# Decoder on one core: four key projections moved from the end of the self-attention to behind the first two value projections of the masked attention

## The chip, the cores and the metric

One core of one Trainium2 chip runs the whole program in one launch. The metric is device microseconds (us) from start to end of an execution. TensorE (PE) has one in-order stream of matmuls, here in fp32: each matmul of the program shows as two records of the profile. PEld is its weight load, which overlaps it. The other engines are VectorE (DVE), ScalarE (ACT), GpSimd (POOL) and the DMA queue of SyncE (SP). They run side by side and wait for each other on semaphores.

## The reference

The program is a two-layer decoder on x (4 x 512 x 256). The part that matters is the first layer's two attentions, for each of four batches:

```python
# self-attention: 16 heads of 64, one zero key and value added
out = softmax(q @ [k;0].T * 64**-0.5) @ [v;0]
x = layernorm(x + out @ W_out + b_out)
# masked attention against ctx: 16 heads of 16
q = x @ Wq.T + bq + pos ;  k = ctx @ Wk.T + bk + pos ;  v = ctx @ Wv.T + bv
s = where(mask == 0, -1e9, q @ k.T / 4)
x = layernorm(x + softmax(s) @ v)
```

The keys and values of the masked attention depend on ctx alone, the queries on the layer norm between the two attentions. Behind these stand a mixture of 8 experts, a four-layer state-space stage, a second cross attention and a quantised gated network; none of their code is touched.

## The kernel before

All matrices lie in SBUF with the features on 128 partitions. One batch has T = 4 tiles of 128 tokens. A loop over the batches runs `attention(b)` and then `project(b + 1)`, which prepares the self-attention of the next batch. The order on each engine is written out by hand; semaphores tie the engines together.

The self-attention (`attend` with AT_A, 32 steps, one tile of two heads each) is a pipeline: scores on TensorE (L1196), maximum on VectorE, exponentials on ScalarE, scaling on GpSimd (L672), transposes on TensorE (L1209, called LAG = 3 steps later), copies of the transposed halves by VectorE (L1660) and ScalarE (L837), and the value products (L1231), which need four transposed steps each. VectorE copies a bank of output out with L1709, and the attention on TensorE ends with a wait for the last of these.

`attend` takes a function `between`. TensorE calls it right after the last transposes and ahead of the last four value products (the last group). Before the change this is `keys`, which issues the four key projections of the masked attention:

```python
if k == n and between is not None:
    between()
```

`pj` (L1169) is a projection: two matmuls over 512 tokens into one of banks 0 to 3, copied out by ScalarE (L812, Identity with a bias). `tm` (L1177) is a projection with tokens on the partitions, into bank 4 or 5 in turn, and waits for the copy out of the unit before the last:

```python
if u >= 2:
    pe.wait_ge(tm_ev, TM(b, u) - 1)
```

After the self-attention TensorE issues four output projections (TM_AO, 8 matmuls each), whose results VectorE adds to x_in (L1728), then the four value projections of the masked attention (TM_BV, 2 matmuls each), numbered BV0 to BV3 below, then eight transposes of the normalised x (`tr`, L1162), and then the four query projections (PJ_BQ). VectorE adds the bias (L1730), runs the layer norm `ln(b, 0)` (L1630, L1634, L1637, L1640), and only then copies the value projections out (L1734). ScalarE's part of the norm is one square root (L816), preceded by a load of its function table, as the exponentials use another table. BV2 waits for the copy of BV0, BV3 for that of BV1.

SP starts the load of the mask (L500) when the self-attention's value products are done, and the loads of the next batch's x and ctx (L484, L485) when the four output projections have been copied out. Neither waits for the keys.

Of the kernel before, what the change touches and what calls it, by code (L numbers as in the profile page):

```python
# [35 lines left out]
PJ_A, PJ_BK, PJ_BQ, PJ_EK, PJ_EV, PJ_EQ, PJ_L1, PJ_N = 0, 16, 20, 24, 26, 28, 30, 38  # L36
# [3 lines left out]
AT_A, AT_B, AT_E, AT_N = 0, 32, 64, 80  # L40
OT_A, OT_B, OT_E, OT_N = 0, 8, 12, 14
# [62 lines left out]
def place(count, b, u, m):  # L104
    return count(b, u) % m if isinstance(b, Two) else u % m
# [37 lines left out]
def decoder(nc, d, out):  # L143
# [11 lines left out]
    with ExitStack() as ctx:  # L155
# [104 lines left out]
        def wv(at, kc, n):  # L260
            return AR[:, at:at + kc * n].rearrange("p (c n) -> p c n", c=kc)
# [4 lines left out]
        CT = ar([P, KC, S])  # L266
# [3 lines left out]
        probs = ar([P, 4, 2, 512])  # L270
        pT = [ar([P, 2, 4, 512]) for k in range(2)]
        a_qT = ar([P, 8, 512])
        b_kT_at = ar.at
        a_kT = ar([P, 8, 512])
# [9 lines left out]
        a_V = ar([P, T, F])  # L284
# [158 lines left out]
        wbq, wbk, wbv = wv(W_BQ, KC, 512), wv(W_BK, KC, 512), wv(W_BV, KC, D)  # L443
# [349 lines left out]
        def _(act):  # L793
# [10 lines left out]
            def tr_ev(u, dst, base):  # L804

                act.wait_ge(tr_ps, TR(base, u) + 1)
                act.activation(dst, PS[:, 6, :].rearrange("p (t q) -> p t q", q=P)  # L807
                               if len(dst.shape) == 3 else PS[:, 6, :], ACT.Copy).then_inc(tr_a, 1)

            def pj(b, u, dst, func=ACT.Copy, scale=1.0, bias=0.0):  # L810
                act.wait_ge(pj_ps, PJ(b, u) + 1)
                act.activation(dst, PS[:, place(PJ, b, u, 4), :], func, bias=bias, scale=scale).then_inc(pj_ev, 1)  # L812

            def ln(b, i):
                act.wait_ge(ln_mv, LN(b, i) + 1)
                act.activation(std[:], mv[:, :, 1], ACT.Sqrt, bias=epsc[:, 0:1]).then_inc(ln_std, 1)  # L816

            def attend(b, at, n, src, per, probs, pT):
                s0, g0 = AT(b, at), GT(b, at // 4)
                def exps(i):  # L820
                    s = s0 + i
                    act.wait_ge(smax, s + 1)
                    if i >= 4:
                        act.wait_ge(pt_ps, s - 3)
                        act.wait_ge(den_ok, s - 3)
                    for q in range(2):
                        ins = act.activation(probs[:, i % 4, q, :], src(i, q), ACT.Exp, scale=-1.0 if at == AT_B else 1.0,  # L827
                                             bias=nm[:, i % 4, q:q + 1], accum_out=sm[:, i % 4, q:q + 1])
                    if per == 2:
                        ins = act.activation(e0[:, i % 4, :], nm[:, i % 4, :], ACT.Exp)  # L830
                    ins.then_inc(probs_ok, 1)

                def copy(k):
                    act.wait_ge(pt_ps, s0 + k + 1)
                    if k % 4 == 0 and k >= 8:
                        act.wait_ge(av, g0 + k // 4 - 1)
                    act.activation(part_of(pT, k, 1, per), PS[:, 5, :].rearrange("p (c q) -> p c q", q=P), ACT.Copy).then_inc(pt_a, 1)  # L837

                for i in range(n + LAG):
                    if at == AT_B and i % 2 == 0:  # L840
                        for k in (i - LAG, i - LAG + 1):
                            if 0 <= k < n:
                                copy(k)
                    if i >= LAG and at != AT_B:
                        copy(i - LAG)
                    if i < n:
                        exps(i)
# [17 lines left out]
            def attention(b):  # L865
                attend(b, AT_A, 32, lambda i, q: PS[:, 2 * (i % 2) + q, :], 2, probs, pT)
                for c in range(4):
                    pj(b, PJ_BK + c, b_kT[:, c, :], ACT.Identity, bias=cols[:, C_BK + c:C_BK + c + 1])
                ln(b, 0)
                tr_ev(TR_LNA, XT[:, 0, :], b)  # L870

                for c in range(4):
                    pj(b, PJ_BQ + c, b_qT[:, c, :], ACT.Identity, 0.25, cols[:, C_BQ + c:C_BQ + c + 1])
                attend(b, AT_B, 32, lambda i, q: b_S[:, i % 2, q, :], 4, probs, pT)
                ln(b, 1)
                tr_ev(TR_LNB, XT[:, 0, :], b)

            project(0)
            with act.Fori(0, B - 1) as b:
                attention(b)  # L880
                project(b + 1, b)
            attention(B - 1)
            gate_exp(B - 1)

# [265 lines left out]
        def _(pe):  # L1150
# [3 lines left out]
            def tr(b, u, src, c0=0, ln=None):  # L1154
                if u:
                    pe.wait_ge(tr_a, TR(b, u))
                    pe.wait_ge(tr_v, TR(b, u))
                for t in range(T):
                    if ln is not None:
                        pe.wait_ge(ln_out, LN(b, ln) * T + t + 1)  # L1160
                    for c in range(KC):
                        ins = pe.transpose(PS[:, 6 + c, t * P:(t + 1) * P], src[:, t, (c0 + c) * P:(c0 + c + 1) * P], ident[:])  # L1162
                ins.then_inc(tr_ps, 1)

            def pj(b, u, w, xT, c, kc=KC, p0=0):
                if u - p0 >= 4 or isinstance(b, Two):
                    pe.wait_ge(pj_ev, PJ(b, u) - 3)
                for k in range(kc):
                    ins = pe.matmul(PS[:, place(PJ, b, u, 4), :], w[:, k, c * P:(c + 1) * P], xT[:, k, :],  # L1169
                                    start=k == 0, stop=k == kc - 1)  # L1170
                ins.then_inc(pj_ps, 1)

            def tm(b, u, xT, t, w, kc=KC, n0=0, n=D):
                if u >= 2:
                    pe.wait_ge(tm_ev, TM(b, u) - 1)
                for k in range(kc):
                    ins = pe.matmul(PS[:, 4 + place(TM, b, u, 2), 0:n], xT[:, k, t * P:(t + 1) * P], w[:, k, n0:n0 + n],  # L1177
                                    start=k == 0, stop=k == kc - 1)
                ins.then_inc(tm_ps, 1)
# [91 lines left out]
            def attention(b):  # L1271
                pe.wait_ge(pj_ev, PJ.one(b, PJ_BK))
                pe.wait_ge(tm_ev, TM.one(b, TM_AO))
                pe.wait_ge(ld_b, 64)

                def keys():
                    for c in range(4):
                        pj(b, PJ_BK + c, wbk, CT, c)

                attend(b, AT_A, 32, a_qT, a_kT, a_V, 2, OT_A, False, probs, pT, keys)  # L1280
                for t in range(T):
                    tm(b, TM_AO + t, a_oT, t, waout, kc=FC)

                for t in range(T):
                    tm(b, TM_BV + t, CT, t, wbv)
                tr(b, TR_LNA, X, ln=0)
                pe.wait_ge(tr_a, TR.one(b, TR_LNB))
                pe.wait_ge(tr_v, TR.one(b, TR_LNB))

                for c in range(4):  # L1290
                    pj(b, PJ_BQ + c, wbq, XT, c)
                pe.wait_ge(pj_ev, PJ.one(b, PJ_EK))
                pe.wait_ge(tm_ev, TM.one(b, TM_EV))
                attend(b, AT_B, 32, b_qT, b_kT, b_V, 4, OT_B, True, probs, pT)
                for t in range(T):
                    for m in range(4):
                        ins = pe.transpose(PS[:, t, m * P:(m + 1) * P], b_oT[:, m, t * P:(t + 1) * P], ident[:])
                    ins.then_inc(bo_ps, 1)
                tr(b, TR_LNB, X, ln=1)
                pe.wait_ge(tr_a, TR.one(b, TR_CB))  # L1300
                pe.wait_ge(tr_v, TR.one(b, TR_CB))

                for t in range(T):
                    for k in range(KC):
                        ins = pe.matmul(PS[:, 4, t * NE:(t + 1) * NE], XT[:, k, t * P:(t + 1) * P], gateW[:, k, :],
                                        start=k == 0, stop=k == KC - 1)
                ins.then_inc(gate_ps, 1)

            project(0)
            with pe.Fori(0, B - 1) as b:  # L1310
                attention(b)
                project(b + 1, b)
            attention(B - 1)
            rank(B - 1)
            pe.wait_ge(wred_ok, 1)
# [916 lines left out]
```

## Time and profile before

| | us |
|---|---|
| median of 3 runs | 4511.87 (4507.68 to 4519.54) |
| profiled execution | 4511.59 |
| span in its profile | 4509.9 |
| mean granted TensorE clock | 0.934 |
| TensorE busy | 3857.7 |
| VectorE busy | 3081.9 |
| key projections start, batches 0 to 3 | 169.73, 479.23, 789.82, 1098.88 |
| query projections start, batches 0 to 3 | 207.16, 517.47, 828.07, 1136.00 |

Times in rows are microseconds from the start of the span. A row of the timeline gives start, length, engine, line of the kernel, operation, output and input, count, and in brackets the idle time of the engine before it and who ended it. Ends of matmuls are modelled, so starts are the better marks.

### The profile page before, as it was taken

The page shows a single profiled execution, that of the slowest core. Times are in us where ns is not written, and L with a number is a line of the kernel's source. Part 1 is how long each engine was busy: PE and PEld are TensorE (multiplying, and loading weights), DVE is VectorE, ACT ScalarE, POOL GpSimd, SP SyncE. Part 2 cuts the span into 40 slices and gives each one's busy share as a digit, 9 for nine tenths or more (in the row PEclk, how much of TensorE's full clock was granted, in tenths as well). Part 3 has the DMA queues.
Part 4 walks back from the last instruction along what each step waited for, and adds up shares of the span by engine and source line. Part 5 has one row for each costly group of instructions (what it writes and reads, how often), then busy time and mean ns, then how long its engine had stood idle before and what let it go on. Part 6 is the DMA issues. An engine that isn't in the chain of part 4 may idle for free.

```text
span 4509.9 us, 47995 instructions
## 1 busy us (share of the span) xinstructions
PE 3857.7 (86%) x15752; PEld 2038.4 (45%) x15760; DVE 3081.9 (68%) x4131; ACT 2302.7 (51%) x4201; POOL 2285.2 (51%) x1206
## 2 busy tenths in 40 slices
PE   7879889789769995799999999999999987887786
PEld 3444444444459993233333333433333333444443
DVE  3566447446631112599999999999999998546646
ACT  4455455445622222666667666666666663332432
POOL 2354345334500003578888787778887785230220
PEclk9999999999979997899999999999999999788788
DMA  6000000000068883011111111111111120000000
GB/s 223 19 6 11 19 15 2 19 15 10 1 254 317 314 315 113 26 35 34 48 34 40 36 48 33 40 36 34 48 36 38 36 91 25 8 10 10 10 1 10
DMA packets 102383, 272.99 MB, mean 61 GB/s; under 512 B 9776, under 2 KB 55728, under 8 KB 96400
## 3 DMA queue, kind: packets, MB, share of 16 engines
q1 hardware_dynamic: 97216, 256.75, 16.5%
q0 software_dynamic: 4944, 13.51, 0.9%
q8 instruction: 110, 1.80, 0.2%
q14 instruction: 113, 0.93, 0.1%
HBM read 237.32 MB, written 32.90 MB: 60 GB/s over the span
## 4 chain that ended last, share of the span: by engine, by line
PE 37%; DVE 18%; POOL 18%; issue 16%; ACT 9%; SPq 1%; DMA 0%; POOLq 0%; another core or an unknown queue 0%; DVEq 0%; ACTq 0%
POOL AR L672 11%; DVE AR L1940 8%; PE PS L1450 8%; PE PS L1337 6%; DVE PS L1934 4%; PE PS L1393 4%; POOL AR L773 3%; PE PS L1347 3%; PE PS L1364 3%; PE PS L1169 3%; ACT AR L1035 2%; PE PS L1177 2%; PE PS L1196 2%; PE PS L1209 2%; PE PS L1443 1%
## 5 line engine op out<-in xcount | busy, mean ns | idle before, releaser
L773 POOL TENSOR_TENSOR AR<-AR 128x1024 f32<-128x1024 f32 x512 | 1217.6, 2384 | 414.8 <-DVE AR L1940 338.4
L1940 DVE TENSOR_TENSOR_SCAN AR<-AR,PS 128x1024 f32<-128x1024 f32 x512 | 1170.4, 2286 | 17.6
L672 POOL TENSOR_TENSOR AR<-AR,rden 128x1024 f32<-128x1024 f32 x320 | 606.2, 1895 | 1002.0 <-DVE rden L1671 935.1
L1450 PE MATMUL PS<-AR,ident 128*128 128x512 f32 x2048 | 1024.6, 628 | 33.4 <-POOL AR L773 33.3
L1035 ACT ACTIVATE AR<-AR,mcol 128x511 f32<-128x511 f32 x1024 | 668.1, 712 | 140.9 <-DVE AR L1940 138.6
L1934 DVE TENSOR_TENSOR PS<-AR,PS 128x1024 f32<-128x1024 f32 x512 | 627.9, 1226 | 79.0 <-PE PS L1435 60.0
L1450 PEld LDWEIGHTS PS<-AR,ident 128*128 128x128 f32 x2048 | 371.6, 194 | 481.1 <-issue 413.5
L1209 PE MATMUL PS<-ident,AR 128*128 128x128 f32 x2560 | 379.4, 295 | 107.0 <-POOL AR L672 92.1
L1209 PEld LDWEIGHTS PS<-ident,AR 128*128 128x128 f32 x2560 | 299.6, 150 | 354.0 <-POOL AR L672 221.8
L1196 PE MATMUL PS<-AR 32*128 32x512 f32 (+1 forms) x1280 | 318.3, 710 | 45.1 <-ACT e L830 11.7
L837 ACT ACTIVATE AR<-PS 128x512 f32<-128x512 f32 x320 | 189.7, 593 | 302.5 <-PE PS L1209 301.8
L827 ACT ACTIVATE AR<-PS,nm 128x512 f32<-128x512 f32 x384 | 259.6, 685 | 95.5 <-DVE nm L1696 74.0
L1169 PE MATMUL PS<-AR 128*128 128x512 f32 x608 | 284.7, 627 | 13.2 <-ACT AR L807 4.5
L1364 PE MATMUL PS<-AR 128*128 128x512 f32 x512 | 260.5, 633 | 39.5 <-ACT AR L1013 24.1
L1337 PE MATMUL PS<-AR 128*128 128x128 f32 x2496 | 286.9, 276 | 8.5 <-ACT AR L893 8.5
L1337 PEld LDWEIGHTS PS<-AR 128*128 128x128 f32 x2496 | 286.6, 193 | 10.9 <-ACT AR L893 8.9
L1660 DVE COPY AR<-PS 128x512 f32<-128x512 f32 x320 | 219.9, 687 | 86.5 <-PE PS L1209 85.5
L1177 PE MATMUL PS<-AR 128*128 128x256 f32 (+1 forms) x896 | 236.6, 424 | 32.5 <-DVE AR L1734 18.0
L1231 PE MATMUL PS<-AR 128*32 128x256 f32 (+1 forms) x2048 | 256.1, 452 | 2.3 <-DVE AR L1660 1.2
L1393 PE MATMUL PS<-AR 128*128 128x512 f32 x512 | 242.3, 596 | 6.3 <-ACT AR L939 4.0
L1882 DVE TENSOR_TENSOR AR<-PS,AR 128x512 f32<-128x512 f32 x78 | 54.0, 692 | 271.0 <-ACT AR L902 271.0
L1689 DVE CUSTOM_DVE_ANT_0 AR<-PS,AR 128x512 f32<-128x512 f32 x256 | 169.4, 683 | 102.0 <-PE PS L1196 98.2
(259 smaller groups left out, 4682.5 us busy)
## 6 DMA issues: line engine op xcount, KB each, us to landing
AR<-in_xw SPq DMA_DIRECT2D x39, 3072.0 KB, 10.5
AR<-mid_cs SPq DMA_DIRECT2D x256, 256.0 KB, 3.3
mid_xs<-AR SPq DMA_DIRECT2D x32, 512.0 KB, 7.7
AR<-mid_xs SPq DMA_DIRECT2D x39, 128.0 KB, 9.6
mid_ys<-AR POOLq DMA_DIRECT2D x39, 128.0 KB, 7.9
AR<-in_ctx SPq DMA_DIRECT2D x8, 512.0 KB, 4.9
AR<-in_mask SPq DMA_DIRECT2D x4, 1024.0 KB, 5.4
mid_x<-AR SPq DMA_DIRECT2D x8, 512.0 KB, 3.0
```

The lines of the kernel that those rows point to most:

```text
L672: pool.tensor_tensor(probs[:, i % 4], probs[:, i % 4], rden[:, i % 4, :].rearrange("p (q o) -> p q o", o=1).to_broadcast([P, 2, 512]), ALU ...
L773: pool.tensor_tensor(m_HC[:, W % 3], m_H[:, W % 3, :].rearrange("p (c s) -> p c s", c=2), m_cb[:, n % 4:n % 4 + 1, :].to_broadcast([P, 2, ...
L1035: ins = act.activation(m_dA[:, W % 4, c, 1:512], m_dl[i % 2][:, cc, 1:512], ACT.Exp, scale=mcol[:, i // B, at:at + 1])
L1169: ins = pe.matmul(PS[:, place(PJ, b, u, 4), :], w[:, k, c * P:(c + 1) * P], xT[:, k, :], start=k == 0, stop=k == kc - 1)
L1196: ins = pe.matmul(PS[:, 2 * (e % 2) + q, :], qT[r:r + wide, h // per, t * P:(t + 1) * P], kT[r:r + wide, h // per, :], start=True, stop=True)
L1209: ins = pe.transpose(PS[:, 4 + q, c * P:(c + 1) * P], probs[:, k % 4, q, c * P:(c + 1) * P], ident[:])
L1337: ins = pe.matmul(PS[:, bank, f * P:(f + 1) * P], w[:, kc, f0:f0 + P], x_T[:, kc, :], start=kc == 0, stop=kc == KC - 1)
L1364: ins = pe.matmul(bank, mWin[:, k, c * P:(c + 1) * P], m_hT[:, k, :], start=k == 0, stop=k == KC - 1)
L1393: ins = pe.matmul(bank, dgc[:, 4 * c + k, :], m_xi[:, c, k:k + 512], start=k == 0, stop=k == 3)
L1450: ins = pe.matmul(PS[:, 2 * hf + c, :], ident[:], m_HC[:, W % 3, c, :], start=False, stop=n == NS - 1)
L1934: v.tensor_tensor(PS[:, 4:6, :], m_du[i % 2][:, 2 * hf:2 * hf + 2, :], PS[:, 6:7, :].to_broadcast([P, 2, 512]), ALU.mult).then_inc(d_bx, 1)
L1940: v.tensor_tensor_scan(m_H[:, W % 3, :], m_dA[:, W % 4].rearrange("p c s -> p (c s)"), PS[:, 4:6, :].rearrange("p c s -> p (c s)"), 0.0, A ...
```

## The change

TensorE no longer issues the four key projections within the self-attention. It issues them between BV1 and BV2. ScalarE, whose order must match, copies out the first key projection, then does its part of the layer norm, then copies out the other three.

```diff
@@ scalar: attention(b)
                 for c in range(4):
                     pj(b, PJ_BK + c, b_kT[:, c, :], ACT.Identity, bias=cols[:, C_BK + c:C_BK + c + 1])
-                ln(b, 0)
+                    if c == 0:
+                        ln(b, 0)
                 tr_ev(TR_LNA, XT[:, 0, :], b)
@@ tensor: attention(b)
-                def keys():
-                    for c in range(4):
-                        pj(b, PJ_BK + c, wbk, CT, c)
-
-                attend(b, AT_A, 32, a_qT, a_kT, a_V, 2, OT_A, False, probs, pT, keys)
+                attend(b, AT_A, 32, a_qT, a_kT, a_V, 2, OT_A, False, probs, pT)
                 for t in range(T):
                     tm(b, TM_AO + t, a_oT, t, waout, kc=FC)
 
                 for t in range(T):
                     tm(b, TM_BV + t, CT, t, wbv)
+                    if t == 1:
+                        for c in range(4):
+                            pj(b, PJ_BK + c, wbk, CT, c)
                 tr(b, TR_LNA, X, ln=0)
```

## Rows read from the trace of the kernel before

**Rows 1.** The page: span, busy time and share of each engine.
```profile
span 4509.9 us, 47995 instructions
PE 3857.7 (86%) x15752; PEld 2038.4 (45%) x15760; DVE 3081.9 (68%) x4131; ACT 2302.7 (51%) x4201; POOL 2285.2 (51%) x1206
```

**Rows 2.** Waits, 168 to 216 us (batch 0): total, times, longest.
```profile
DVE AR L1709 <- PE PS L1231: 10.3, 2, 10.0
PE PS L1177 <- DVE AR L1734: 4.5, 1, 4.5
```

**Rows 3.** Timeline of batch 0, end of the self-attention.
```profile
168.72 1.08 PE L1231 MATMUL PS<-AR 128*64 128x512 f32 x4
168.83 0.69 DVE L1660 COPY AR<-PS 128x512 f32<-128x512 f32 x1 [1.50 <-PE PS L1209]
169.73 7.13 PE L1169 MATMUL PS<-AR 128*128 128x512 f32 x16
171.75 0.69 ACT L812 ACTIVATE AR<-PS,cols 128x512 f32<-128x512 f32 x1 [2.33 <-PE PS L1169]
173.47 0.69 ACT L812 ACTIVATE AR<-PS,cols 128x512 f32<-128x512 f32 x1 [1.03 <-PE PS L1169]
176.80 3.65 PE L1231 MATMUL PS<-AR 128*64 128x512 f32 x16
180.50 0.69 DVE L1709 COPY AR<-PS 128x512 f32<-128x512 f32 x1 [9.96 <-PE PS L1231]
```

**Rows 4.** Timeline of batch 0, output projections to query projections.
```profile
181.32 15.80 PE L1177 MATMUL PS<-AR 128*128 128x256 f32 x72 [0.87 <-DVE AR L1709]
185.07 0.42 DVE L1728 TENSOR_TENSOR AR<-PS,AR 128x256 f32<-128x256 f32 x1 [3.88 <-PE PS L1177]
188.53 0.42 DVE L1728 TENSOR_TENSOR AR<-PS,AR 128x256 f32<-128x256 f32 x1 [3.03 <-PE PS L1177]
199.12 0.30 ACT L816 ACTIVATE std<-mv,epsc 128x4 f32<-128x4 f32 x1 [20.22 <-DVE mv L1634]
201.17 0.76 DVE L1734 TENSOR_TENSOR AR<-PS,AR 128x256 f32<-128x256 f32 x2
201.65 3.26 PE L1177 MATMUL PS<-AR 128*128 128x256 f32 x8 [4.53 <-DVE AR L1734]
207.16 7.13 PE L1169 MATMUL PS<-AR 128*128 128x512 f32 x16 [0.97 <-DVE AR L1621]
```

**Rows 5.** Windows, batch 0: PE, PEld, DVE, ACT, POOL busy, granted clock, DMA share, GB/s.
```profile
198.00:202.00 4.00, 0.35 (x2) 0.33 (x3) 3.25 (x13) 0.30 (x1) 0.00 (x0) 1.00 0.71 245
202.00:206.00 4.00, 4.00 (x16) 3.28 (x14) 0.85 (x2) 0.00 (x0) 0.00 (x0) 0.57 0.00 0
...
124.00:168.00 44.00, 43.63 (x232) 19.67 (x232) 33.17 (x73) 27.57 (x80) 27.76 (x15) 1.00 0.00 1
```

**Rows 6.** Timeline of batches 1 and 3, the same stretch.
```profile
511.14 3.78 PE L1177 MATMUL PS<-AR 128*128 128x256 f32 x8 [4.52 <-DVE AR L1734]
517.47 7.13 PE L1169 MATMUL PS<-AR 128*128 128x512 f32 x16 [0.96 <-DVE AR L1621]
1130.63 3.67 PE L1177 MATMUL PS<-AR 128*128 128x256 f32 x8 [4.43 <-DVE AR L1734]
1134.13 1.04 PE L1162 MATMUL PS<-ident,AR 128*128 128x128 f32 x8
1136.00 7.10 PE L1169 MATMUL PS<-AR 128*128 128x512 f32 x16 [0.83 <-ACT AR L807]
```

**Rows 7.** Timeline of ScalarE around another table load.
```profile
340.80 0.60 ACT L812 ACTIVATE AR<-PS 128x512 f32<-128x512 f32 x1 [1.12 <-PE PS L1169]
341.41 1.28 ACT L862 ACT_TABLE_LOAD   x1
342.70 0.23 ACT L862 ACTIVATE g_t<-g_t 128x32 f32<-128x32 f32 x1
```

**Rows 8.** Line L1169, start to 225 us: ns min/median/max of a record.
```profile
L1169 PE MATMUL PS<-AR x96: 592/592/1192, 20.8 to 213.7; 128*128 128x512 f32 x96
```

## The prediction

> **What bounds the kernel now.** I read the page first [rows 1]: TensorE is the busiest engine with 86% of the span, but that is an average over five very different stages, so it says nothing yet about this change. The chain that ended last is no help in this stretch either: it puts the 52 us between two scalings of GpSimd down to "issue". So I went to the waits of the stretch from the end of one attention to the start of the next, then to its timeline, in which the order can be followed.
>
> The waits show two places where an engine stands still for long behind another [rows 2]: VectorE 10.0 us for TensorE, ahead of the last copy of the self-attention's output, and TensorE 4.5 us for VectorE, ahead of BV2.
>
> The first is explained by the timeline [rows 3]. The last transposed half is copied by VectorE from 168.83 for 0.69 us, to 169.52. That is all that the last group of value products needs, and TensorE has issued the group before it by then. But at 169.73 it starts the keys, 16 records that take until 176.80, and only then the last value products. VectorE's copy, the output projections, the layer norm and everything behind them stand behind that group. So the keys are wholly on the path here, though no one needs them before the next attention. Batches 0 to 3 repeat it alike; the row of batch 0 stands for four.
>
> The second is in the next stretch [rows 4]. TensorE starts the output projections at 181.32. Their results are copied out 3.45 us apart (185.07, 188.53), which is 16 records, so a record costs 0.216 us. The group has 72 records (64 of the output projections, 8 of BV0 and BV1), so TensorE has issued it all at 181.32 + 72 x 0.216 = 196.85. I call this moment T0. BV2 starts at 201.65, T0 + 4.80, because VectorE copies BV0 out only behind the layer norm. The whole rest is one chain: ScalarE's root at 199.12, normalisation, copy of BV0 from 201.17, BV2, BV3, transposes, queries at 207.16.
>
> The clock belongs to it [rows 5]. While TensorE is idle, from 198 to 202 us, the granted clock is still 1.00; in the next 4 us it is 0.57, so it has fallen to the lower of its two levels, 1.2 GHz, behind an idle of 4.5 us. The 8 records of BV2 and BV3, which would take 1.73 us, take over 3 us. From the start of BV2 to the start of the queries it is 5.51 us in batch 0, 6.33 us in batch 1 [rows 4, 6], as much in batch 2, and 5.37 us in batch 3 (1130.63 to 1136.00), on average 5.9 us.
>
> **What goes away.** The keys leave the path at the end of the self-attention: 176.80 - 169.73 = 7.07 us per batch. What else could hold the last value products there? Only the two copies of transposed halves, over at 169.52, and TensorE's own order. The idle from such a copy to a matmul behind it is small: BV2 starts at 201.65 behind a copy that begins at 201.17 and takes 0.42. So the group starts between 169.6 and 169.8, and the saving is between 7.0 and 7.15 us; I take 7.07. Nothing reads the keys until the masked attention, and there is no DMA in the part that moves: 8 matmuls (16 records, 16 weight loads) and 4 copies on ScalarE. Of SP's queue, the mask's load is released by the end of the value products and so comes 7 us earlier, as its reader does; the loads of x and ctx follow the output projections and shift with them.
>
> **What is added.** The keys now start at T0 instead of an idle of 4.8 us. I take the same 7.07 us for them, so BV2 starts at T0 + 7.07 if TensorE sets it. I check the other chain, since ScalarE's root now stands behind the copy of the first key. That copy starts 2.02 us behind the first key record (171.75 against 169.73) and takes 0.69, the table load behind it 1.28, so the root can start at T0 + 4.0, against T0 + 2.27 before. From the root to BV2 it was 201.65 - 199.12 = 2.53 us. VectorE would so release BV2 at T0 + 6.5: the norm comes 1.7 us later than before, and this is hidden under the keys with only 0.5 us to spare. Behind ScalarE's root wait the copies of keys 1 to 3; they come 1.72 us apart and no one waits for them but the masked attention. The copies use Identity, and in the timeline the query copies, which stand behind the root, run without a table load in front of them, so none is added. VectorE's copies of BV0 and BV1, and the normalised x for the transposes, are in time by the same sum.
>
> The clock pays a part back. TensorE has no idle from the output projections to BV2, so I expect it to stay at 2.4 GHz. BV2 and BV3 then take 8 x 0.216 = 1.73 us, and from the transposes to the queries it is 1136.00 - 1134.13 = 1.87 us, from batch 3, in which the transposes already ran fast [rows 6]. That is 3.60 us instead of 5.9.
>
> The sum of this stretch from T0 to the queries: before 4.8 + 5.9 = 10.7 us; after 7.07 + 3.60 = 10.67 us. The keys fit into the idle and the clock's loss, and cost nothing. What is left is the 7.07 us of the first place, four times: 28.3 us. If that cover were gone, that is, with the clock low from BV2 on, the second stretch would take 7.07 + 5.9 = 12.97 us, and 2.3 us per batch come back.
>
> What a switch of ScalarE's table costs is seen in full at another place [rows 7]: a copy ends at 341.40, the load starts at 341.41 and takes 1.28 us, and the function starts at 342.70, so nothing but the load itself lies between. A rule of the Trainium skill speaks against this reckoning. The Trainium skill (ScalarE: Activation LUTs, "What ACT_TABLE_LOAD costs") adds a drain of about 1.38 us to every switch. By it the root would start at T0 + 5.4 and BV2 at T0 + 7.9, 0.8 to 0.9 us behind the keys, and the sum would be some 25 us. Rows 7 contradict it for this kernel.
>
> **The rivals.**
>
> *The clock falls anyway* behind the keys. For it: it fell in all four batches at this place, and is low again early in the masked attention. Against: it fell behind an idle that is now filled. Time: 4 x (7.07 - 2.3) = 19.1 us gained, 4492.5.
>
> *ScalarE's root becomes the bound*, since it stands behind a copy and a table load that used to be long done. For it: only 0.5 us are to spare, on modelled ends. Against: rows 7. If the switch costs the length of a second load, 1.28 us, BV2 comes 0.8 us late: 28.3 - 3.2 = 25.1 us gained, 4486.5. The drain of the Trainium skill's page, above, would be one way to this case.
>
> *The change doesn't shorten the path*: the last value products wait for something that the keys hide. The seven us would turn up as idle ahead of L1231. Against: both copies are over at 169.52. No change, 4511.6.
>
> *Slower*: the low clock comes earlier, ahead of or in the keys. They are 7 us of unbroken matmul, which now no longer stand ahead of the output projections, where TensorE idles for 0.87 us. Against: from 124 to 168 us TensorE is busy for 43.6 of 44 us at clock 1.00 [rows 5], and at 1.00 through the output projections. A record of a projection takes 592 ns, and up to 1192 in the slow level [rows 8], twice as much. With all keys at half clock they cost 6.9 us more, with BV2 to the queries at the old 5.9: 13.97 + 5.9 = 19.9 against 10.7, 9.2 lost against 7.07 won, 2.1 us worse per batch, 4520. It decides from the point where some 7 us of full-clock work run at half clock; were part of the output projections slow too, each 3.45 us of them would cost as much again.
>
> **How the numbers follow.** The profiled execution is 4511.59 us for a span of 4509.9, and the median of the three runs is 4511.87, so the sum can be made against either: 4511.6 - 28.3 = 4483.3. The likeliest case has 74 in 100. Its own range is some 6 us to either side: the placing of the clock's falls later in the layer differs from batch to batch (queries of batch 2 to those of batch 3 are 307.9 us apart, others 310.3 and 310.6, so it is worth up to 2.7 us a batch), and the runs before lie 12 us apart. The clock falling anyway 8, ScalarE's root 6, no change 4, the slower case 8, half of it within 0.3%. A measurement of this kernel can tell about 0.3% (13.5 us) from nothing. The first three are faster: 88 in 100; within 0.3%: 8; slower: 4. The range for 8 in 10 goes from 4475 to 4496, and takes in the first three.
>
> **What would show it.** In the profile after, L1231's last group starts about 1 us behind the group before it, and VectorE's wait ahead of the last L1709 falls from 9.96 us to about 2.9. L1177's group of BV2 shows no idle of 4.5 us; L1169 x16 stands in front of it. The root L816 starts about 4 us behind the keys' start, directly behind its table load, which now lies behind the first key copy. The clock from BV2 to the queries is 1.00, and BV2 to queries takes 3.6 us. The queries of batches 0 to 3 start earlier by about 7, 14, 21 and 28 us. The prediction is wrong if BV2 waits visibly for VectorE, if the clock is 0.5 to 0.6 in these 4 us, or if an idle appears ahead of the last L1231.

## The result and the profile after

The changed kernel takes 4484.32 us (median of 4 runs, 4481.83 to 4489.70), beside 4515.70 us (4507.68 to 4519.95) of the kernel before. The medians are 31.4 us apart. The ratio on record is 0.9938, with a 95% interval from 0.9922 to 0.9955. It is not the quotient of the two medians (0.9931), but the interval holds both. By the ratio the change is worth 28 us (20 to 35), so the gain is clear of noise. The forecast was 4483.3. Its span is 26.8 us shorter:

```profile
span 4483.1 us, 48003 instructions
```

The timeline of batch 0 answers to [rows 3] and [rows 4]. In the changed file the line numbers of TensorE are one higher (L1196 is L1197, L1169 is L1170, L1177 is L1178, L1162 is L1163), and the value products are L1232. In the other runs they move by a few lines too.

```profile
167.08 4.69 PE L1232 MATMUL PS<-AR 128*64 128x512 f32 x20
168.21 0.69 DVE L1709 COPY AR<-PS 128x512 f32<-128x512 f32 x1 [0.33 <-PE PS L1232]
171.82 0.69 DVE L1709 COPY AR<-PS 128x512 f32<-128x512 f32 x1 [2.92 <-PE PS L1232]
...
172.64 15.80 PE L1178 MATMUL PS<-AR 128*128 128x256 f32 x72 [0.86 <-DVE AR L1709]
...
188.28 7.03 PE L1170 MATMUL PS<-AR 128*128 128x512 f32 x16
...
190.20 0.69 ACT L812 ACTIVATE AR<-PS,cols 128x512 f32<-128x512 f32 x1 [22.41 <-PE PS L1170]
190.90 1.28 ACT L816 ACT_TABLE_LOAD   x1
192.20 0.30 ACT L816 ACTIVATE std<-mv,epsc 128x4 f32<-128x4 f32 x1
...
194.25 0.76 DVE L1734 TENSOR_TENSOR AR<-PS,AR 128x256 f32<-128x256 f32 x2
195.15 1.89 PE L1178 MATMUL PS<-AR 128*128 128x256 f32 x8
...
196.88 1.04 PE L1163 MATMUL PS<-ident,AR 128*128 128x128 f32 x8
...
198.88 7.13 PE L1170 MATMUL PS<-AR 128*128 128x512 f32 x16 [0.96 <-DVE AR L1621]
```

Read it from the top. The last two groups of value products now run as one piece of 20 records: nothing stands between them. VectorE's wait for the last one is 2.92 us, against 9.96 in [rows 3]: 7.04 us less. T0, the moment at which TensorE has issued BV1, is 172.64 + 15.53 = 188.17 (15.53 us are 72 records of 3.45 / 16 us, as in the prediction), and the keys start at 188.28. BV2 starts at 195.15, T0 + 6.98, with no idle in brackets, against 201.65 and 4.53 us of idle in [rows 4]. From BV2 to the queries it is 3.73 us instead of 5.51. ScalarE's root starts directly behind its table load, and that directly behind the copy of the first key.

The granted clock, which was 0.57 from 202 to 206 us in [rows 5], is 1.00 in the same part of the work:

```profile
192.00:196.00 4.00, 4.00 (x12) 2.09 (x11) 2.32 (x7) 2.40 (x5) 0.00 (x0) 1.00 0.06 18
196.00:200.00 4.00, 3.04 (x16) 2.16 (x15) 2.67 (x4) 0.63 (x2) 0.00 (x0) 1.00 0.01 4
```

The four batches, from the start of the output projections to the first scores of the masked attention, in us, worked out from the starts in the timelines:

| batch | 0 | 1 | 2 | 3 | sum |
|---|---|---|---|---|---|
| before | 33.82 | 34.64 | 34.65 | 33.50 | 136.61 |
| changed | 34.22 | 34.22 | 34.22 | 33.99 | 136.65 |

So eight matmuls per batch, 7 us of TensorE, were added to this stretch for 0.04 us in all. Before, the stretch differs by up to 1.2 us between batches, by where the clock fell and rose; now it hardly does.

**The balance of the span.** At the end of the self-attention 7.04 us were won in three batches (VectorE's wait falls from 9.96 to 2.92 us) and 7.19 in the last (to 2.77): 28.3 us. Batch 0 also reached this point 1.6 us earlier in the profiled execution (the start of the output projections is 8.68 us earlier, the change explains 7.04). That makes 29.9 us, and 26.8 were seen. Two rows have the rest. From the first masked scores to the root of the second norm batch 0 took 105.6 us (206.86 to 312.48) against 103.7 before (215.14 to 318.86), 1.9 us more. And the transposes behind the second norm ran at the slow clock from their start in batches 1 and 2, 0.56 us more each. Both are places where the clock is low for some us in either kernel, and the runs below, `after_again` above all, bear on whether the change is the cause.

### The profile page after: what moved, and what is told of

Its sections match the earlier page's. It is cut to its first block, busy times and chain, and to the rows that moved or that the text cites. A ratio compares the mean times of both kernels' runs of the same rounds, so it can differ in the third digit from the quotient of the medians.

```text
span 4483.1 us, 48003 instructions
## 1 busy us (share of the span) xinstructions
PE 3851.2 (86%) x15760; PEld 2035.4 (45%) x15760; DVE 3082.2 (69%) x4131; ACT 2302.9 (51%) x4201; POOL 2285.0 (51%) x1206
## 4 chain that ended last, share of the span: by engine, by line
PE 37%; POOL 18%; DVE 18%; issue 15%; ACT 9%; SPq 1%; DMA 0%; POOLq 0%; DVEq 0%; ACTq 0%
POOL AR L672 11%; PE PS L1450 8%; DVE AR L1940 7%; PE PS L1337 6%; DVE PS L1934 4%; PE PS L1393 4%; POOL AR L773 3%; PE PS L1347 3%; PE PS L1364 3%; PE PS L1170 3%; ACT AR L1036 3%; PE PS L1178 2%; PE PS L1197 2%; PE PS L1210 2%; PE PS L1443 1%
## 5 line engine op out<-in xcount | busy, mean ns | idle before, releaser
L1197 PE MATMUL PS<-AR 32*128 32x512 f32 (+1 forms) x1280 | 317.3, 709 | 45.0 <-ACT AR L827 11.5
L1170 PE MATMUL PS<-AR 128*128 128x512 f32 x608 | 285.1, 627 | 13.2 <-ACT AR L807 4.5
L1232 PE MATMUL PS<-AR 128*32 128x256 f32 (+1 forms) x2048 | 255.8, 452 | 2.3 <-DVE AR L1660 1.2
L1178 PE MATMUL PS<-AR 128*128 128x256 f32 (+1 forms) x896 | 229.7, 415 | 14.5 <-DVE AR L1709 5.0
```

What stands on the lines that cost most here:

```text
L1197: ins = pe.matmul(PS[:, 2 * (e % 2) + q, :], qT[r:r + wide, h // per, t * P:(t + 1) * P], kT[r:r + wide, h // per, :], start=True, stop=True)
```

## The experiments

A ratio is always to the kernel before on the same chip, as the chips differ: the kernel before has a median of 4503.3 us beside keys_twice, keys_out, root_last and two_moved, 4510.5 beside warm_norm, key_behind, root_first and warm_both, and 4502.5 beside first_behind, best and after_again. An interval of 0.9920 to 0.9953 is 15 us wide, so differences of a few us are read from the rows.

| run | median us | ratio (95% interval) |
|---|---|---|
| changed kernel | 4484.32 | 0.9938 (0.9922 to 0.9955) |
| keys_twice | 4505.42 | 1.0005 (0.9995 to 1.0015) |
| keys_out | 4474.25 | 0.9937 (0.9920 to 0.9953) |
| root_last | 4502.14 | 0.9997 (0.9988 to 1.0007) |
| two_moved | 4485.10 | 0.9963 (0.9949 to 0.9977) |
| warm_norm | 4473.99 | 0.9921 (0.9898 to 0.9945) |
| key_behind | 4482.59 | 0.9932 (0.9909 to 0.9955) |
| root_first | 4484.39 | 0.9942 (0.9921 to 0.9962) |
| warm_both | 4466.98 | 0.9905 (0.9883 to 0.9928) |
| first_behind | 4473.71 | 0.9938 (0.9921 to 0.9954) |
| best | 4448.92 | 0.9879 (0.9863 to 0.9896) |
| after_again | 4475.45 | 0.9943 (0.9926 to 0.9959) |

### keys_twice: the new place alone

```diff
                     tm(b, TM_BV + t, CT, t, wbv)
+                    if t == 1:
+                        pe.wait_ge(pj_ev, PJ.one(b, PJ_BQ))
+                        for c in range(4):
+                            for k in range(KC):
+                                pe.matmul(PS[:, c, :], wbk[:, k, c * P:(c + 1) * P], CT[:, k, :],
+                                          start=k == 0, stop=k == KC - 1)
```

> The kernel before, with the eight key matmuls issued a second time between BV1 and BV2, into the same banks, their results unused. Only the second place is tested. Theory (the 7 us fit into an idle of 4.8 us plus the 2.2 us that the clock gives back): T0 to the queries 10.7 us as before, the whole within 2 us of before, clock 1.00 from BV2 to the queries. Rival 1 (only the idle counts, the clock would stay low behind the keys too): 2.3 us more per batch, 9 us slower. Rival 2 (matmuls put there simply cost their 7 us): 28 us slower.

Eight more matmuls per batch, 28 us of work in all, change the time by a ratio of 1.0005, and by 7 us at the most (1.0015). The timeline shows why; L1290 are the repeated keys:

```profile
197.22 7.03 PE L1290 MATMUL PS<-AR 128*128 128x512 f32 x16
...
204.09 1.89 PE L1177 MATMUL PS<-AR 128*128 128x256 f32 x8
205.82 1.04 PE L1162 MATMUL PS<-ident,AR 128*128 128x128 f32 x8
207.82 7.13 PE L1169 MATMUL PS<-AR 128*128 128x512 f32 x16 [0.96 <-DVE AR L1627]
```

BV2 starts 2.2 us later than the idle would allow, and makes this good by 3.73 us instead of 5.9 to the queries. From the output projections to the masked scores it is 34.22, 34.22, 34.21 and 33.99 us, as in the changed kernel. Rival 1, by which the clock gives nothing back, would need 2.3 us more in each. In this kernel the path ahead is the old one, so the new place is shown to be free by itself: the four stretches take 136.6 us, as they do before.

### keys_out: the old place alone

```diff
                     if t == 1:
-                        for c in range(4):
-                            pj(b, PJ_BK + c, wbk, CT, c)
+                        pe.sem_inc(pj_ps, 4)
```

> The changed kernel without the eight key matmuls anywhere: TensorE only counts up the semaphore between BV1 and BV2, ScalarE still copies four (stale) banks, so the masked attention uses wrong keys. Theory (moved keys are free): the idle of 4.8 us and the low clock behind it come back, T0 to the queries 10.3 to 11.1 us as before the change, the whole within 3 us of the changed kernel's 4484. Rival 1 (the keys overfill the idle and the clock is high either way): 8.5 instead of 10.7 us per batch, 8.7 us faster than the changed kernel, 4476. Rival 2 (the keys cost their 7 us in the new place): 28 us faster, 4456.

This kernel leaves the keys out, so its masked attention works with wrong ones. The ratio is 0.9937, that of the changed kernel. As far as the interval tells, to leave the keys out altogether brings no more than to move them. The idle and the slow clock are back:

```profile
194.76 3.78 PE L1178 MATMUL PS<-AR 128*128 128x256 f32 x8 [4.52 <-DVE AR L1733]
198.33 1.90 PE L1163 MATMUL PS<-ident,AR 128*128 128x128 f32 x8
201.20 7.13 PE L1170 MATMUL PS<-AR 128*128 128x512 f32 x16 [0.96 <-DVE AR L1620]
```

BV2 to the queries is 6.44 us here, and from the output projections to the masked scores it is 34.74, 34.75, 34.71 and 33.50 us: a little more, on average, than with the keys in place.

### root_last: how late the norm may be

```diff
                     pj(b, PJ_BK + c, b_kT[:, c, :], ACT.Identity, bias=cols[:, C_BK + c:C_BK + c + 1])
-                    if c == 0:
-                        ln(b, 0)
+                ln(b, 0)
```

> The changed kernel with ScalarE's old order: all four key copies, then the square root of the layer norm. Theory (the norm is hidden under the keys with 0.5 us to spare, and becomes the bound as soon as it is later): the root starts at T0 + 9.3 us instead of T0 + 4.0, BV2 at T0 + 11.8 behind an idle of some 4.8 us, the clock falls behind it, 5.9 instead of 3.7 us to the queries: 7 us more per batch, 28 us more than the changed kernel, 4512, as much as before the change. Rival (ScalarE's order does not matter, since only TensorE's order makes the gain): 4484. Rival 2 (the idle comes, but the clock stays high): 4.8 us per batch, 4503.

The whole gain is gone, with TensorE's order as in the changed kernel: ratio 0.9997.

```profile
196.76 1.28 ACT L816 ACT_TABLE_LOAD   x1
198.06 0.30 ACT L816 ACTIVATE std<-mv,epsc 128x4 f32<-128x4 f32 x1
...
200.59 3.55 PE L1177 MATMUL PS<-AR 128*128 128x256 f32 x8 [4.56 <-DVE AR L1733]
...
206.10 7.13 PE L1169 MATMUL PS<-AR 128*128 128x512 f32 x16 [0.96 <-DVE AR L1620]
```

T0 is 173.35 + 15.53 = 188.88, so the root starts at T0 + 9.2 and BV2 at T0 + 11.7, as reckoned. The idle of 4.56 us brings the slow clock back: from BV2 to the queries it is 5.5 us in batch 0, against 3.73 in the changed kernel. The stretch to the masked scores is 40.74, 41.67, 41.61 and 40.41 us, 6.9 us more per batch than in the changed kernel and 27.8 in the four. So without the change's move on ScalarE, the move on TensorE gains nothing.

### root_first: whether the root is the bound

```diff
-                for c in range(4):
-                    pj(b, PJ_BK + c, b_kT[:, c, :], ACT.Identity, bias=cols[:, C_BK + c:C_BK + c + 1])
-                    if c == 0:
-                        ln(b, 0)
+                ln(b, 0)
+                for c in range(4):
+                    pj(b, PJ_BK + c, b_kT[:, c, :], ACT.Identity, bias=cols[:, C_BK + c:C_BK + c + 1])
```

> The changed kernel with ScalarE's root ahead of all four key copies. Theory (TensorE's keys set BV2, the root had 0.5 us to spare): the root starts at T0 + 2.3 instead of T0 + 4.0, nothing behind BV2 moves, the time is that of the changed kernel, 4484. Rival (BV2 was held by VectorE's chain after all): BV2 earlier than T0 + 6.9, up to 2 us per batch faster.

```profile
192.16 0.30 ACT L816 ACTIVATE std<-mv,epsc 128x4 f32<-128x4 f32 x1 [21.36 <-DVE mv L1633]
...
196.86 1.89 PE L1177 MATMUL PS<-AR 128*128 128x256 f32 x8
```

The output projections start at 174.36, so T0 is 189.89: the root is at T0 + 2.3, 1.8 us earlier than in the changed kernel, and BV2 at T0 + 6.97, as there. The stretch to the masked scores is 34.22, 34.22, 34.22 and 33.99 us, and the ratio 0.9942. The rival, an earlier BV2, did not occur: in the changed kernel the keys set BV2, and the root is hidden.

### key_behind and first_behind: how much is to spare

The first moves key 3 behind the transposes:

```diff
                     if t == 1:
-                        for c in range(4):
+                        for c in range(3):
                             pj(b, PJ_BK + c, wbk, CT, c)
                 tr(b, TR_LNA, X, ln=0)
+                pj(b, PJ_BK + 3, wbk, CT, 3)
```

with ScalarE's copy of key 3 behind `tr_ev(TR_LNA, ...)`. The second also puts the root ahead of all key copies.

> The changed kernel with key 3 behind the transposes of the normalised x, where TensorE idles 0.97 us for their copies; keys 0 to 2 between BV1 and BV2. Theory (keys beyond the idle cost their full time): BV2 at T0 + 5.3 instead of T0 + 7.0, key 3 fills the 0.97 us and costs some 0.8 more, so T0 to the queries 9.8 instead of 10.7: 0.9 us per batch, 3.6 us faster than the changed kernel, 4480, too little for the time to tell but plain in the rows. Rival (VectorE's chain releases BV2 only at T0 + 6.5, as the root stands behind the first key copy): BV2 at T0 + 6.5, and T0 to the queries 11.0, 1 us slower than the changed kernel.

```profile
193.09 0.30 ACT L816 ACTIVATE std<-mv,epsc 128x4 f32<-128x4 f32 x1
...
195.62 1.99 PE L1179 MATMUL PS<-AR 128*128 128x256 f32 x8 [1.13 <-DVE AR L1736]
```

My own theory missed and its rival held. T0 is 189.07; BV2 starts at T0 + 6.55 behind an idle of 1.13 us for VectorE, not at T0 + 5.3. From the output projections to the masked scores it is 34.38 us, 0.16 more than in the changed kernel, and 0.8 us more over the four batches, where the rival had 1. With a shorter filling the root behind the first key copy is the bound at once. That also measures what the prediction had as 0.5 us to spare: 6.98 - 6.55 = 0.43 us.

> Key 3 behind the transposes of the normalised x, and ScalarE's root ahead of all key copies. Theory (VectorE's chain released BV2 at T0 + 6.55 when key 3 stood behind alone, because the root stood behind a key copy): the root starts at T0 + 2.3, BV2 at T0 + 5.3, set by three keys, T0 to the queries 9.8 instead of 10.7 us, 0.9 us per batch, 3.6 us in all. Rival (something else holds BV2): BV2 at T0 + 6.5, no gain.

```profile
191.83 0.30 ACT L816 ACTIVATE std<-mv,epsc 128x4 f32<-128x4 f32 x1 [21.36 <-DVE mv L1635]
...
194.82 1.89 PE L1178 MATMUL PS<-AR 128*128 128x256 f32 x8
```

T0 is 189.56, BV2 at T0 + 5.26 without idle, and the stretch to the masked scores is 32.99 us in three batches and 32.92 in the last, 1.2 us less than in the changed kernel, where 0.9 was expected. By the time (4473.71 beside 4475.45 of the changed kernel on the same chip) this can't be told from nothing; only the rows show it. The 4.7 us of the four batches are in part taken back later: batches 1 and 2 took 105.6 us from the first masked scores to the second root, 1.6 more each than in after_again.

### two_moved: an idle that is partly filled

```diff
                 def keys():
-                    for c in range(4):
+                    for c in range(2):
                         pj(b, PJ_BK + c, wbk, CT, c)
...
                     tm(b, TM_BV + t, CT, t, wbv)
+                    if t == 1:
+                        for c in range(2, 4):
+                            pj(b, PJ_BK + c, wbk, CT, c)
```

> Keys 0 and 1 stay at the end of the self-attention, keys 2 and 3 move between BV1 and BV2; ScalarE takes the root between the copies of key 1 and key 2. Theory: 3.5 us leave the first place; in the second, two keys fill 3.5 of 4.8 us, an idle of 1.3 us is left, behind which the clock stays high: T0 to the queries 4.8 + 3.7 = 8.5 us against 10.7, so 2.2 us more are won there. Together 5.7 us per batch, 23 us faster than before, 4489 to 4492. Rival (the clock falls behind 1.3 us of idle too): only the 3.5 us, 14 us faster than before, 4501. Rival 2 (half the keys, half of the gain) gives the same 14 us but by other rows; the clock from BV2 to the queries tells.

```profile
169.97 3.70 PE L1170 MATMUL PS<-AR 128*128 128x512 f32 x8
...
173.60 3.65 PE L1232 MATMUL PS<-AR 128*64 128x512 f32 x16
...
198.45 1.99 PE L1178 MATMUL PS<-AR 128*128 128x256 f32 x8 [1.09 <-DVE AR L1738]
200.28 1.04 PE L1163 MATMUL PS<-ident,AR 128*128 128x128 f32 x8
202.28 7.13 PE L1170 MATMUL PS<-AR 128*128 128x512 f32 x16 [0.96 <-DVE AR L1625]
```

At the place itself the theory holds: two keys cost 3.63 us ahead (169.97 to 173.60), 3.44 us less than the four in [rows 3], an idle of 1.09 us is left, and the clock behind it is high (transposes 1.04 us, granted clock 1.00 from 198 to 206 us). The stretch is 32.14 us in two batches, 32.18 and 31.82, on average 2.1 us less than before or in the changed kernel. That adds up to 22 us. The time shows 17 (0.9963, that is 10 to 23 us), between the two expectations. In its profile the first masked scores to the second root took 105.25 us in batch 3 instead of 104.0, and of the gain 4 us are missing between the second root of one batch and the output projections of the next (170.96, 169.28 and 167.44 us, against 171.96, 171.88 and 170.26 before, less 3.44 each). The slow clock stands there for a while in every kernel here. So the rows decide between the expectations, and the time alone would not.

### after_again: the changed kernel on another chip

> The changed kernel as it is, once more, for a second profile on another chip. Theory (what differed by 1.9 us between the queries of batch 0 and the second norm was the place where the low clock fell, not the change): T0 to the queries 10.7 us in all batches again, and the 1.6 us gone or in another batch. Rival (it belongs to the change): 105.6 us from the first masked scores to the second root in batch 0 again.

The ratio is 0.9943. The stretch is 34.21, 34.22, 34.21 and 33.99 us again. From the first masked scores to the second root it is 104.06, 104.04, 104.04 and 104.01 us: the 105.6 of the first profile is gone. Across the kernels with this stretch of code untouched the value is 103.7, 104.0 to 104.1, 105.3 or 105.6 us, in differing batches. The granted clock in the 25 us from the first masked scores goes with it. It is 0.73 in batch 0 of the first profile (105.6 us), 0.80 in its batch 1 (104.1), and 0.86 in batch 0 of the kernel before (103.7), the last line:

```profile
207.00:232.00 25.00, 17.48 (x104) 9.53 (x104) 14.76 (x45) 15.94 (x39) 12.99 (x7) 0.73 0.00 1
512.00:537.00 25.00, 16.93 (x110) 9.68 (x103) 16.00 (x49) 15.56 (x39) 13.35 (x8) 0.80 0.01 1
...
215.10:240.10 25.00, 17.23 (x116) 9.45 (x120) 15.76 (x49) 16.22 (x40) 13.34 (x8) 0.86 0.00 1
```

It is 0.73 too in batches 1 and 2 of first_behind (105.6 us) and in batch 3 of two_moved (105.3), 0.80 in batch 0 of after_again (104.1), and 0.86 in batch 3 of root_last (103.7). So the 1.9 us of batch 0 come from how long the low clock lasts there, which differs between profiles of one kernel, and not from the change. The second row of the balance moved too: the 0.56 us behind the second norm stand in batches 0 and 1 here instead of 1 and 2, and in keys_twice in batches 0, 1 and 2. The kernel before has them in none; whether the change makes them more frequent, one profile of it can't tell.

### warm_norm, warm_both and best: the same reasoning elsewhere

The times between places here and below are worked out from the starts in the timelines. If work in an idle is free and keeps the clock, then matmuls whose results no one uses should gain time by themselves. The place is the second norm of the changed kernel:

```profile
313.49 1.41 PE L1163 MATMUL PS<-ident,AR 128*128 128x128 f32 x8 [3.48 <-DVE AR L1640]
315.84 3.55 PE L1305 MATMUL PS<-gateW,AR 128*128 128x8 f32 x16 [0.94 <-DVE AR L1621]
319.25 1.95 PE L1163 MATMUL PS<-ident,AR 128*128 128x128 f32 x8
322.46 1.94 PE L1163 MATMUL PS<-ident,AR 128*128 128x128 f32 x8 [1.27 <-ACT AR L853]
325.62 8.76 PE L1170 MATMUL PS<-AR 128*128 128x512 f32 x16 [1.22 <-ACT AR L807]
```

Behind 3.48 us of idle the clock is 0.50 from 316 to 328 us.

```diff
                     ins.then_inc(bo_ps, 1)
+                for c in range(4):
+                    pe.matmul(PS[:, 5, :], ident[:], CT[:, c % 2, :], start=True, stop=True)
```

> The changed kernel with four filler matmuls (ident by CT into bank 5, results unused, 8 records, some 3.4 us) behind the output transposes of the masked attention, in TensorE's idle of 3.5 us for the second layer norm. The same reasoning at a second place, without any gain from a shorter path. Theory (a filled idle keeps the clock): in the changed kernel the granted clock is 0.5 for some 14 us behind this idle (transposes 1.97 us for 8, gate 3.55, transposes 1.95 and 1.94, first queries and keys of the next batch 8.76 instead of 7.13). With the clock at 1.00 this is worth 5 to 6 us in each of three batches and 2 in the last: 15 to 20 us faster than the changed kernel, 4464 to 4469. Rival (the clock falls behind the later idles of 0.9 to 1.3 us anyway): the first transposes only, 1 us per batch, 4480. Rival 2 (filler is late work and delays the transposes): slower by up to 1 us per batch.

```profile
315.95 1.92 PE L1307 MATMUL PS<-gateW,AR 128*128 128x8 f32 x16 [0.94 <-DVE AR L1623]
317.72 1.07 PE L1163 MATMUL PS<-ident,AR 128*128 128x128 f32 x8
320.06 1.94 PE L1163 MATMUL PS<-ident,AR 128*128 128x128 f32 x8 [1.27 <-ACT AR L853]
323.22 10.01 PE L1170 MATMUL PS<-AR 128*128 128x512 f32 x16 [1.22 <-ACT AR L807]
```

Gate and first transposes are fast now, but the next transposes and the projections are not: 1.94 us as before, and 10.01 instead of 8.76. The granted clock of this run shows where it falls, behind the idle of 0.94 us and as that of 1.27 us begins:

```profile
314.00:318.80 4.80, 3.85 (x31) 3.16 (x30) 1.96 (x7) 0.60 (x1) 0.00 (x0) 1.00 0.32 113
318.80:329.00 10.20, 7.71 (x15) 4.09 (x16) 2.74 (x15) 2.77 (x5) 0.00 (x0) 0.50 0.00 0
```

From the second root to the next output projections batches 0 to 2 win 1.5, 1.7 and 3.3 us, 6.6 together, not 15. On the same chip it is 10 us faster than root_first, whose TensorE does the changed kernel's work. That lies between the expectation (15 to 20 us) and its rival (some 4). Much of the slow stretch only moved on.

warm_both adds three more behind the first scores of the masked attention:

```diff
                         scored(i)
+                        if i == 0:
+                            for c in range(3):
+                                pe.matmul(PS[:, 7, :], ident[:], CT[:, c % 2, :], start=True, stop=True)
```

> As the kernel with filler in the second norm, and three more filler matmuls (2.6 us, bank 7) behind the first scores of the masked attention, where TensorE idles 2.8 us. Theory (the clock falls for this idle): the low clock in the first 20 us of the masked attention goes or is shorter; from the queries to the output transposes it was 109.2 us in batch 0 and 107.6 in batches 1 and 2 of the changed kernel; 1 to 3 us per batch less, 4 to 12 us in all beside the other filler. Rival (later idles of 1 to 3 us in the filling of the pipeline lower the clock as well, or GpSimd's scaling sets the pace anyway): no more than 1 us per batch.

```profile
207.30:211.30 4.00, 3.20 (x13) 1.38 (x14) 1.86 (x7) 2.48 (x3) 0.00 (x0) 1.00 0.00 0
211.30:215.30 4.00, 2.63 (x17) 1.09 (x16) 2.21 (x10) 2.41 (x8) 2.72 (x2) 1.00 0.01 2
215.30:219.30 4.00, 3.12 (x15) 2.17 (x17) 2.76 (x7) 3.65 (x10) 2.39 (x2) 0.59 0.00 0
```

The clock stays high for 8 us behind the first masked scores and then falls to 0.59 all the same, later than in the changed kernel. The first masked scores to the second root take 103.2, 104.6, 103.2 and 101.7 us instead of 105.6, 104.1, 104.1 and 104.1: 5 us in all, and 7 by the medians of warm_norm and warm_both. Against the usual 104.05 us it is less: 0.9, -0.6, 0.9 and 2.4 us. So only batch 3 gains what was expected (1 to 3 us), two batches stay below it, as the rival had it, and batch 1 loses.

`best` adds to the last two the order of first_behind, and one filler each in the idles to which the slow clock had moved:

```diff
                 tr(b, TR_LNB, X, ln=1)
+                pe.matmul(PS[:, 5, :], ident[:], CT[:, 0, :], start=True, stop=True)
...
                 tr(b, TR_X, x_in)
+                if prior is not None:
+                    pe.matmul(PS[:, 5, :], ident[:], CT[:, 0, :], start=True, stop=True)
                 tr(b, TR_C, ctx_tok)
+                if prior is not None:
+                    pe.matmul(PS[:, 5, :], ident[:], XT[:, 0, :], start=True, stop=True)
```

> As the kernel with the root first and key 3 behind, with filler matmuls (results unused) in all idle places found: four in the second norm, three behind the first masked scores, and one each ahead of the gate, between the transposes of the next x and ctx, and ahead of the next projections. Theory (with filler in the second norm alone the low clock only moved to the next idles of 0.9 to 1.3 us; filled too, it goes): clock 1.00 from the second norm to the end of the next projections, transposes 1.04 us instead of 1.94, first projections 7.13 instead of 8.6 to 10.0, 4 us more in each of three batches; with the other parts 15 us less than the kernel with two fillers, ratio to before 0.987. Rival (a filler that misses its idle is work on the path): each costs up to 0.9 us, and the time stays at the ratio 0.990.

```profile
314.98 1.07 PE L1163 MATMUL PS<-ident,AR 128*128 128x128 f32 x8
...
317.32 1.07 PE L1163 MATMUL PS<-ident,AR 128*128 128x128 f32 x8 [0.41 <-ACT AR L853]
...
319.60 7.11 PE L1170 MATMUL PS<-AR 128*128 128x512 f32 x16 [0.36 <-issue]
```

The projections take 7.11 us, the transposes 1.07, and the granted clock is 1.00 in every window of 4 us from 300 to 328 us. From the second root to the next output projections it is 160.2, 160.6 and 158.3 us, against 164.9, 165.4 and 163.7 in the changed kernel. The ratio is 0.9879, where 0.987 was expected and 0.990 by the rival. That is 26.5 us less than the changed kernel on the same chip (4448.92 beside 4475.45), and 24.8 less than first_behind, from which it differs by the fillers alone: 10 matmuls more per batch (8 in the last) whose results no one reads.

## Why the prediction was right

**What goes away** was put at 7.07 us per batch; the wait of VectorE shows 7.04 and in the last batch 7.19. It rested on the reading that the value products wait only for copies over by 169.52 and for TensorE's own order. That they now follow the group before without a gap shows it, and keys_out gets the same gain without any keys.

**What is added** was BV2 at T0 + 7.07; it came at T0 + 6.98. The root was put at T0 + 4.0 and came at T0 + 4.03; VectorE's release of BV2 was put at T0 + 6.5, and key_behind measured T0 + 6.55. The rival of ScalarE's root was so near because 0.43 us were all there was to spare, and root_last shows what it would have cost in full: the whole gain.

**The clock** was to pay back 2.3 us per batch: 3.60 us from BV2 to the queries instead of 5.9; it was 3.73 in three batches and 3.59 in the last. The prediction took its 1.87 us from the transposes to the queries from batch 3, and in the others it is 2.00. BV2 comes 0.09 us earlier than reckoned, which makes up for most of that: T0 to the queries was put at 10.67 us, and is 10.70. The rival that it falls anyway is excluded by the windows of the changed kernel, and keys_twice shows this term apart from the first one: 28 us of added work, ratio 1.0005. The slower rival, a low clock ahead of the keys or in them, did not occur: the output projections take 15.80 us as before, and the keys 6.87 us from their start to BV2.

**The table switch.** The load at 190.90 starts when the copy ends and the root follows 0.02 us behind it. The drain of about 1.38 us that the Trainium skill (ScalarE: Activation LUTs, "What ACT_TABLE_LOAD costs") adds is not seen in this place either, and the trace disagrees with that figure here: the root starts at T0 + 4.03, not at T0 + 5.4.

**The sum** of 28.3 us stands beside 26.8 in the span, 28 by the ratio and 31.4 between the medians. The queries start 8.3, 13.8, 20.7 and 26.8 us earlier; about 7, 14, 21 and 28 were forecast. What the sum left out, the place of the slow clock later in the layer, was -3.0 us, against 1.6 us by which batch 0 came earlier. By after_again the 1.9 us of batch 0 are not the change's; for the 1.1 us behind the second norm that is likely and not shown. The start of batch 0 differs as much within one kernel: its output projections start at 172.64 us in the first profile and at 175.16 in after_again. That these terms nearly cancel is luck, and so is the median within 1 us of the forecast, as the four runs of the changed kernel lie 8 us apart. Two expectations were wrong in kind, both for later runs: that key 3 could go behind the transposes with the root left where it was (key_behind), and that filler in the longest idle would keep the clock through the shorter ones behind it (warm_norm).

## What to carry to other kernels

Work that stands on the path only because it was written there is found by looking at what the next engine waits for, not at how busy the engine is: here the engine at 86% had 7 us of work in the wrong place and 4.8 us of idle 27 us later. An idle is worth more than its length where the clock falls behind it, so that work somewhat longer than the idle can still be free. When work moves into another engine's wait, write out that engine's own order too: with ScalarE's root behind all four copies the same move on TensorE gained nothing (0.9997).

## What the runs showed of the hardware

- A clock kept high over one idle fell behind the next, shorter ones. With 3.5 us of idle filled (warm_norm, batch 0), the granted clock was 1.00 past an idle of 0.94 us and 0.50 from 318.8 us on, through idles of 1.27 and 1.22 us. In two_moved, with matmuls close together between them, it stayed at 1.00 over idles of 1.09 and 0.96 us. In best, with the idles behind the second norm filled but for 0.41 us or less, it was 1.00 from 300 to 328 us. Why it fell in the one case and not in the other, no run here shows.
- Matmuls that compute nothing of use made the kernel faster: with two fillers 4466.98 us beside 4484.39 of the same work without them on one chip (warm_both, root_first), with five places filled 4448.92 beside 4473.71 (best, first_behind).
- The same stretch of code, from the first masked scores to the second root, took 103.7, 104.0 to 104.1 or 105.3 to 105.6 us in different batches and kernels in which nothing of it was changed, with a granted clock of 0.86, 0.80 or 0.73 in its first 25 us. So a difference of 2 us in a stretch of 105 is not to be put down to an edit elsewhere from one profile, before the clock of the stretch has been looked at.
